# Start-up loads in two groups, a bias folded later, and experts' matrices in five slots, three tiles ahead

## The chip, the core and the metric

The kernel runs on one core of one Trainium2 chip. The metric is device time in microseconds (us) of one execution. All arrays are float32 in HBM; a few operands are bfloat16 in SBUF.

## The reference

The input is `x`, 32 sequences of 128 tokens with 128 features, and a context `ctx_1024` of the same shape. Four layers follow, each an attention and a feed-forward part, both added to `x`:

```python
x = x + xattn_l(layernorm(x), ctx, ...)     # l = 0..3
x = x + ffn_l(layernorm(x), ...)
```

- Layer 0 and 1: cross attention, 16 heads of 8 (causal in layer 0); then a mixture of 8 experts, of which each token takes 2 (128 to 512 to 128; ReLU, then GELU with biases).
- Layer 2: a decoder block (self attention, cross attention, a plain 128-512-128 network, three layer norms); then "gated attention": 8 experts that are attentions themselves, 2 for each token, with an output bias `ob` for each expert and a value bias `vb`. Attention weights add up to one, so `vb` goes through the output matrix unchanged: the kernel folds it into `ob` once, `ebias = ob + sum_p vbias_p^T Eo_p`.
- Layer 3: cross attention with rotary positions and a window of 64 tokens; then 8 experts with a gate (SiLU(x G) * (x U)) D, 2 for each token.

## The kernel before, in words

The 32 sequences are two streams, s = 0 and s = 1, of 16 sequences; a step works on a pair of sequences (256 tokens), so each stream has 8 pairs (`PAIRS`). Each stream is a Python generator for each engine. TensorE's generators give each step a cost and a delay; `choose_order` plays them against a model of time, starting stream 1 at `HEAD_START` = 100, and every engine then issues the steps of both streams in that one fixed order. So each engine is one in-order list with both streams interleaved.

Start. SyncE (SP) issues, in order: for both streams the first pair of `x` (`x_first`) and of the context (`c_in`); then 18 loads that all count on one semaphore, `weights_in`: `wproj` (all 52 projection matrices, 3328 KB) first, nine small tables, the masks, then seven tables spread over all partitions (`rows`, 960 KB, among them). TensorE, ScalarE and VectorE begin with a wait for all 18 (lines 338, 1098, 1332). VectorE then clears four PSUM banks and makes bfloat16 copies (lines 1334 to 1339); when `consts_set` is complete TensorE makes the bias fold (line 341, 8 products written as 16 instructions) and VectorE adds it to `ebias` (line 1342); both streams begin behind that. SP waits for `consts_set` too (line 798), since it then sends zeros from SBUF into stream 0's area for sorted rows, `sent` (line 794: four transfers of 2560 KB, `clear`), and only behind those, on the same queue, loads the other 14 sequences of `x` for each stream (line 802, `x_rest`, 896 KB each), and `wf`. VectorE needs `x_rest` early: in the third unit of pair 0's attention, `come` (line 1573) takes the statistics of pair 1 (line 1374).

Mixtures (layers 0, 1, 3; each stream; six in all). Tokens are scattered by expert into `sent`; VectorE makes a plan (`plan`) of 39 tiles (`TILES`) of 128 rows, each with its expert. For each tile SP reads the plan's registers and issues three transfers: the expert's matrices (line 845, `load_expert`: 512, 578 or 384 KB in layers 0, 1, 3), the tile's rows (line 849, `load_rows`, 64 KB) and the finished rows of tile n-2 (line 853, `store_rows`, 64 KB). In step n TensorE turns the rows of tile n (line 527), makes the first products of tile n-1 (`first`, line 535, 8 instructions) and the second ones of tile n-2 (`second`, line 543). VectorE or ScalarE take the results out; VectorE's copy of tile n-2's answer (line 1679 or 1681) releases SP, which then issues the load of tile n+2's expert into slot (n+2) mod 4, the slot that tile n-2 has left. Rows are loaded six tiles ahead. At a mixture's start two experts are loaded as soon as the plan is there (line 839 ff.), and the rows only when all scatters have landed.

After a mixture the answers come back by indirect DMA on GpSimd (line 958, `fetch`) and VectorE adds them (`combine`, line 1451). After the last mixture, stream 1's in layer 3, 8 pairs are fetched and stored; stream 0's last combines are interleaved with that mixture's tiles.

The bias fold is used in line 669, in the gated attention of layer 2.

## Time and profile before

| | |
|---|---|
| median of 3 runs | 3465.97 us (3463.64 to 3470.96) |
| the profiled execution, its own time | 3460.97 us |
| span of its trace | 3459.1 us |
| TensorE matmuls busy | 2811.5 us, 81% of the span |
| VectorE busy | 1986.3 us, 57% |
| ScalarE busy | 1326.2 us, 38% |
| GpSimd busy | 633.1 us, 18% |
| moved by DMA | 217.14 MB, mean 63 GB/s |

The span is 1.9 us shorter than the execution's own time, and that time is 5.0 us under the median. A share of busy time is a mean over very different stages. A "wait" is idle time of an engine just ahead of an instruction, with the event that ended it. "The chain" is the work followed back from the last instruction to what released each step. SPq is SP issuing DMAs. A transfer's bytes are moved by 16 DMA engines; "DMA share" is the mean share of these that is busy, and can be put a little over 1 in short stretches. PEclk is TensorE's granted clock; 1.00 is 2.4 GHz and 0.50 is 1.2 GHz.

### The profile page before, as it was taken

The page shows a single profiled execution, that of the slowest core. Times are in us where ns is not written, and L with a number is a line of the kernel's source. Part 1 is how long each engine was busy: PE and PEld are TensorE (multiplying, and loading weights), DVE is VectorE, ACT ScalarE, POOL GpSimd, SP SyncE. Part 2 cuts the span into 40 slices and gives each one's busy share as a digit, 9 for nine tenths or more (in the row PEclk, how much of TensorE's full clock was granted, in tenths as well). Part 3 has the DMA queues.
Part 4 walks back from the last instruction along what each step waited for, and adds up shares of the span by engine and source line. Part 5 has one row for each costly group of instructions (what it writes and reads, how often), then busy time and mean ns, then how long its engine had stood idle before and what let it go on. Part 6 is the DMA issues. An engine that isn't in the chain of part 4 may idle for free.

```text
span 3459.1 us, 64816 instructions
## 1 busy us (share of the span) xinstructions
PE 2811.5 (81%) x24730; PEld 1999.2 (58%) x24818; DVE 1986.3 (57%) x6642; ACT 1326.2 (38%) x3062; POOL 633.1 (18%) x847
## 2 busy tenths in 40 slices
PE   5888888866687997997988988988988988987852
PEld 2444666633574874664764765755655655656752
DVE  2566445456544355666666666666766766665432
ACT  1344334433474743333333333334334333334421
POOL 0122112223312011121121121111111111110033
PEclk8888998977797998999998999999999999998976
DMA  7300656500373810000000000000000000004464
GB/s 252 113 23 22 182 145 181 154 21 24 106 226 96 242 44 7 3 9 7 3 9 7 3 9 7 3 9 7 3 9 7 3 9 4 3 4 125 116 189 125
DMA packets 146515, 217.14 MB, mean 63 GB/s; under 512 B 20377, under 2 KB 99233, under 8 KB 146081
## 3 DMA queue, kind: packets, MB, share of 16 engines
q1 hardware_dynamic: 133920, 187.80, 17.8%
q0 software_dynamic: 12288, 25.19, 2.4%
q8 instruction: 200, 3.28, 0.4%
q14 instruction: 107, 0.87, 0.1%
HBM read 159.83 MB, written 53.08 MB: 62 GB/s over the span
## 4 chain that ended last, share of the span: by engine, by line
PE 56%; DVE 21%; ACT 10%; issue 6%; DMA 4%; SPq 2%; another core or an unknown queue 2%; POOL 1%; DVEq 0%; POOLq 0%; ACTq 0%
PE bank L442 5%; ACT ex L1132 5%; PE bank L380 5%; DVE mx L1594 4%; PE bank L535 4%; PE bank L617 4%; PE bank L386 4%; PE bank L452 4%; PE bank L599 3%; PE bank L462 3%; PE bank L543 3%; PE bank L371 3%; PE bank L446 3%; DMA expert<-in_moe 3%; PE bank L431 2%
## 5 line engine op out<-in xcount | busy, mean ns | idle before, releaser
L1132 ACT ACTIVATE ex<-bank 128x512 f32<-128x512 f32 x896 | 472.6, 600 | 661.1 <-PE bank L452 431.0
L1594 DVE TENSOR_REDUCE mx<-bank 128x4 bf16<-128x512 f32 x640 | 407.4, 683 | 125.3 <-PE bank L431 67.5
L944 POOL TENSOR_TENSOR rstd<-vare,power 128x2 f32<-128x2 f32 x192 | 135.8, 707 | 1372.9 <-DVE vare L1387 1372.9
L535 PE MATMUL bank<-qm,expert 128*128 128x128 f32 x1872 | 265.1, 287 | 35.6 <-DMA expert<-in_moe 29.4
L1011 POOL TENSOR_TENSOR oT<-oT 128x128 f32<-128x128 f32 x256 | 117.9, 461 | 917.2 <-DVE oT L1713 916.6
L535 PEld LDWEIGHTS bank<-qm,expert 128*128 128x128 f32 x1872 | 239.8, 200 | 51.8 <-DMA expert<-in_moe 39.4
L953 POOL DMA_INDIRECT sent<-tail_tok,pos x192 | 191.3, 996 | 391.5 <-DVE pos L1522 347.1
L380 PE MATMUL bank<-hT,wproj 128*128 128x256 f32 x736 | 242.8, 427 | 23.7 <-ACT hT L1095 8.3
L1586 DVE RECIPROCAL rden<-bank 128x16 f32<-128x16 f32 x160 | 41.0, 256 | 382.9 <-PE bank L471 347.2
L442 PE MATMUL bank<-qm,kf 32*128 32x512 f32 x1280 | 207.4, 710 | 56.8 <-ACT ex L1132 36.0
L617 PEld LDWEIGHTS bank<-ev,ex 128*128 128x128 f32 x2048 | 246.9, 192 | 5.1 <-issue 0.2
L425 PE MATMUL bank<-km,qb 32*128 32x512 bf16 x640 | 141.3, 447 | 133.4 <-DVE logit L1463 33.4
L617 PE MATMUL bank<-ev,ex 128*128 128x65 f32 x2048 | 243.7, 272 | 0.0
L543 PE MATMUL bank<-expert,hid 128*128 128x128 f32 x1560 | 220.4, 281 | 20.7 <-DVE hid L1667 11.4
L452 PEld LDWEIGHTS bank<-identb,mx 128*128 128x128 bf16 x2560 | 160.3, 102 | 89.5 <-issue 58.6
L543 PEld LDWEIGHTS bank<-expert,hid 128*128 128x128 f32 x1560 | 197.2, 195 | 25.6 <-DVE hid L1667 12.2
L462 PE MATMUL bank<-ex,vaug 128*9 128x128 f32 x5120 | 185.2, 275 | 21.4 <-issue 9.9
L371 PE MATMUL bank<-masks,identb 128*128 128x512 bf16 x648 | 179.8, 415 | 20.1 <-issue 11.1
L1699 DVE TENSOR_REDUCE emax<-bank 128x4 bf16<-128x512 f32 x256 | 164.3, 683 | 46.4 <-PE bank L589 46.1
L452 PE MATMUL bank<-identb,mx 128*128 128x128 bf16 x2560 | 179.7, 226 | 9.0 <-DVE mx L1594 9.0
L1091 ACT ACTIVATE oT<-bank 128x512 f32<-128x512 f32 x160 | 96.0, 600 | 194.6 <-PE bank L462 150.3
L425 PEld LDWEIGHTS bank<-km,qb 32*128 32x128 bf16 x640 | 33.9, 93 | 216.6 <-issue 141.0
(207 smaller groups left out, 5051.0 us busy)
## 6 DMA issues: line engine op xcount, KB each, us to landing
expert<-in_moe SPq DMA_DIRECT2D x78, 578.0 KB
expert<-in_moe SPq DMA_DIRECT2D x78, 512.0 KB
expert<-in_moe SPq DMA_DIRECT2D x78, 384.0 KB
sent<-zeros SPq DMA_DIRECT2D x8, 2560.0 KB, 9.1
ex<-sent SPq DMA_DIRECT2D x234, 64.0 KB
answered<-qm SPq DMA_DIRECT2D x234, 64.0 KB
ctxT<-ctx_kept SPq DMA_DIRECT2D x32, 128.0 KB
wproj<-in_wproj SPq DMA_DIRECT2D x1, 3328.0 KB
```

The source lines that it names most:

```text
L371: nc.tensor.matmul(ps[:], identb[:, 0, :], masks[:], start=True, stop=True)
L380: mm = nc.tensor.matmul(ps[:, n * NT:(n + 1) * NT], W(weight), src[:], start=True, stop=True)
L425: mm = nc.tensor.matmul(ps[i][:], qb[s][r, seq(b)], km[s][r, :, seq(b)], start=True, stop=mask is None)
L442: nc.tensor.matmul(ps[j][:], kf[s][band_rows(j), seq(b)], qm[s][band_rows(j), :, seq(b)], start=True, stop=False)
L452: mm = nc.tensor.matmul(ps[j][:, i * P:(i + 1) * P], mx[s][:, b, h:h + 1].to_broadcast([P, P]), identb[:, 1, :], start=False, stop=i == HB ...
L462: mm = nc.tensor.matmul(ps[32 * i:32 * i + D + 1, j * P:(j + 1) * P], vaug[s][:, b, HB * j + i, :], ex[s][:, j, i, :], start=True, stop=True)
L535: mm = nc.tensor.matmul(ps[:, chunk(c)], expert[s][:, t % SLOTS, chunk(c)], t_turned[s][:, t % 2, :], start=True, stop=True)
L543: mm = nc.tensor.matmul(ps[:, 0:P], t_hid[s][:, t % 2, chunk(c)], expert[s][:, t % SLOTS, 512 + c * P:512 + (c + 1) * P], start=c == 0, st ...
L617: mm = nc.tensor.matmul(ps[:, c * (HE + 1):(c + 1) * (HE + 1)], ex[s][:, 2 * (p % 2) + i, 2 * b + j, :], ev[s][:, p % 2, b, i, :], start=T ...
L953: nc.gpsimd.indirect_dma_start(sent[s][:], bass.IndirectOffsetOnAxis(ap=pos[s][:, i, j:j + 1], axis=0), tail_tok[s][:, j // 2, :], None).t ...
L1132: give(nc.scalar.activation(ex[s][:, i], ps[:].rearrange("p (i q) -> p i q", i=4), ACT.Exp, scale=SCALE), *key)
L1594: give(nc.vector.tensor_reduce(mx[s][:, b, HB * i:HB * i + HB], ps[:].rearrange("p (i k) -> p i k", i=HB), AX.X, ALU.max), *k, "s", b, i)
```

## The change

Three parts.

1. SP issues first the first pair of stream 0, then six transfers on a new semaphore `first_weights_in` (`ident`, `band`, `cols`, the masks, the first four projection matrices, 256 KB, and `rows`), then the first pair of stream 1, then the other loads, among them the remaining 48 projection matrices, on `weights_in`. TensorE, ScalarE and VectorE begin after `first_weights_in`. Waits for `weights_in` stand ahead of the first router product on TensorE and ahead of the first gates on VectorE. VectorE clears the PSUM banks before its wait. Bytes, and the number of transfers but for one more, stay the same.
2. The bias fold leaves the start. Stream 0 makes it once behind its mixture of layer 1, in a PSUM bank of the ring "g"; VectorE adds it there.
3. Five slots for experts in place of four, and `EXPERTS_AHEAD = 3`: at a mixture's start three experts are loaded, and after tile n-2's answer is out SP loads the expert of tile n+3 (slot (n+3) mod 5, the slot that tile n-2 has left). The event that releases a load is the same as before.

```diff
--- before.py
+++ after.py
@@ -55,7 +55,8 @@
 PLANNED = -(-TILES // BATCH) * BATCH
 
 MOE_COLS = {0: 512 + CH * P, 1: 512 + CH * P + CH + P, 3: 3 * CH3 * P}
-SLOTS = 4
+SLOTS = 5
+EXPERTS_AHEAD = 3
 
 ROW_SLOTS = 8
 ROWS_AHEAD = 6
@@ -102,7 +103,7 @@
     + [f"{n}{s}_{i}" for n in ("expert_in", "last_in") for s in range(STREAMS) for i in range(SLOTS)] \
     + [f"rows_in{s}_{i}" for s in range(STREAMS) for i in range(ROW_SLOTS)] \
     + [f"rows_out{s}_{i}" for s in range(STREAMS) for i in range(OUT_SLOTS)] \
-    + ["weights_in", "ffn_weights_in", "consts_set", "bias_made", "bias_in", "dve_step"]
+    + ["first_weights_in", "weights_in", "ffn_weights_in", "consts_set", "bias_in", "dve_step"]
 CONSTS = 20
 
 PROJ = ["L0q", "L0k", "L0v", "L0o", "L1q", "L1k", "L1v", "L1o", "L2q1", "L2k1", "L2v1", "L2q2", "L2k2",
@@ -112,6 +113,10 @@
 ROWS = ["L0v", "L0o", "L1v", "L1o", "L2v1", "L2v2", "L3v", "L3o", "g1", "be1", "g2", "be2", "g3", "be3",
         "bf2"]
 ROUTERS = {0: 0, 1: 1, 3: 2}
+FIRST_PROJ = 4
 
 
 class Counts:
@@ -296,10 +301,12 @@
         eq_bf16 = [[eq[s][i].rearrange("p i n -> p (i n)").bitcast(BF16)[:, 1::2].rearrange("p (i n) -> p i n", i=2)
                     for i in range(3)] for s in range(STREAMS)]
 
-        loads = [(wproj, "wproj"), (router, "router"), (rw1, "rw1"), (rw2, "rw2"), (cols, "cols"), (rope, "rope"),
-                 (ident, "ident"), (band, "band"), (ebias, "ebias"), (vbias, "vbias")]
-        spread = [(rows, "rows"), (rrow, "rrow"), (rb2, "rb2"), (tri, "tri"), (region, "region"),
-                  (tile_rows, "tile_rows"), (tile_no, "tile_no")]
+        first_loads = [(ident, "ident"), (band, "band"), (cols, "cols")]
+        n_first = len(first_loads) + 3
+        loads = [(router, "router"), (rw1, "rw1"), (rw2, "rw2"), (rope, "rope"), (ebias, "ebias"), (vbias, "vbias")]
+        spread = [(rrow, "rrow"), (rb2, "rb2"), (tri, "tri"), (region, "region"), (tile_rows, "tile_rows"),
+                  (tile_no, "tile_no")]
         n_loads = len(loads) + len(spread) + 1
         masks_f32 = hid[0][:, 0, 0:3, :].rearrange("p a n -> p (a n)")[:, 0:5 * P].rearrange("p (m k) -> p m k", m=5)
 
@@ -335,12 +342,8 @@
         @block.tensor
         def _(pe):
             w = Counts()
-            pe.wait_ge(sem["weights_in"], 16 * n_loads)
+            pe.wait_ge(sem["first_weights_in"], 16 * n_first)
             pe.wait_ge(sem["consts_set"], CONSTS)
-            for p in range(HP):
-                mm = nc.tensor.matmul(bank[6][0:NE, 0:P], vbias[:, p, :], W(f"Eo{p}"), start=p == 0, stop=p == HP - 1)
-            mm.then_inc(sem["bias_made"], 1)
-            pe.wait_ge(sem["bias_in"], 1)
 
             def open_bank(ring, *key):
                 i, n = banks.fill(ring, key)
@@ -396,6 +399,8 @@
                     turn(t, tail_tok[s], "tT")
 
                 def tail_logits(t):
+                    if w.new("weights_in", 16 * n_loads):
+                        pe.wait_ge(sem["weights_in"], 16 * n_loads)
                     taken(*t, "tT")
                     by_token(t, "logits", router[:, ROUTERS[tail_layer(t[2])], :], attT[s], NE)
 
@@ -663,6 +668,8 @@
                             turn_mixed(n - 3)
                         yield "gated unit", 3.6 if 2 <= n < HP else 2.5 if n <= HP + 1 else 0.3, 0.3 if n <= HP else 1.5
                     taken(*k, "wtsT")
+                    if w.new("bias_in", 1):
+                        pe.wait_ge(sem["bias_in"], 1)
                     taken(*k, f"mixedT{HP - 1}")
                     for b in range(NB):
                         ps = open_bank("g", *k, "out", b)[:, 0:P]
@@ -708,6 +715,11 @@
                 yield from mixture((s, "M", 1))
 
 
+                if s == 0:
+                    ps = open_bank("g", "ebias")
+                    for p in range(HP):
+                        mm = nc.tensor.matmul(ps[0:NE, 0:P], vbias[:, p, :], W(f"Eo{p}"), start=p == 0, stop=p == HP - 1)
+                    filled(mm, "ebias")
                 yield "gather", 0.0, 9.0
                 for i in range(PAIRS):
                     tail = (s, i - 1, "C") if i else None
@@ -780,12 +792,21 @@
         @block.sync
         def _(sp):
             w = Counts()
-            for s in range(STREAMS):
+            def first_pair(s):
                 sp.dma_start(x_tok[s][:, 0:NB, :], x_dram[s, :, 0:NB, :]).then_inc(sem[f"x_first{s}"], 16)
                 sp.dma_start(c_st[s][:], c_dram[s, 0]).then_inc(sem[f"c_in{s}"], 16)
+            first_pair(0)
+            for dst, src in first_loads:
+                sp.dma_start(dst[:], A[src]).then_inc(sem["first_weights_in"], 16)
+            sp.dma_start(masks_f32, A["masks"]).then_inc(sem["first_weights_in"], 16)
+            sp.dma_start(wproj[:, 0:FIRST_PROJ, :], A["wproj"][:, 0:FIRST_PROJ, :]).then_inc(sem["first_weights_in"], 16)
+            sp.dma_start(rows[:], A["rows"].unsqueeze(0).to_broadcast(list(rows.shape)))\
+                .then_inc(sem["first_weights_in"], 16)
+            first_pair(1)
             for dst, src in loads:
                 sp.dma_start(dst[:], A[src]).then_inc(sem["weights_in"], 16)
-            sp.dma_start(masks_f32, A["masks"]).then_inc(sem["weights_in"], 16)
+            sp.dma_start(wproj[:, FIRST_PROJ:, :], A["wproj"][:, FIRST_PROJ:, :]).then_inc(sem["weights_in"], 16)
             for dst, src in spread:
                 sp.dma_start(dst[:], A[src].unsqueeze(0).to_broadcast(list(dst.shape))).then_inc(sem["weights_in"], 16)
 
@@ -856,7 +877,7 @@
                     at = {}
                     sp.wait_ge(sem[f"plan_ready{s}"], w.next(f"plan_ready{s}"))
                     read_plan(0)
-                    for t in range(2):
+                    for t in range(EXPERTS_AHEAD):
                         load_expert(t)
                     sp.wait_ge(sem[f"scattered{s}"], sent_off)
                     read_plan(BATCH)
@@ -866,8 +887,8 @@
                     for n in range(TILES + 2):
                         if n >= 2:
                             taken(*k, "y", n - 2)
-                        if n + 2 < TILES:
-                            load_expert(n + 2)
+                        if n + EXPERTS_AHEAD < TILES:
+                            load_expert(n + EXPERTS_AHEAD)
                         if n >= 2:
                             store_rows(n - 2)
                         if n + ROWS_AHEAD < TILES:
@@ -1074,7 +1095,7 @@
         @block.scalar
         def _(act):
             w = Counts()
-            act.wait_ge(sem["weights_in"], 16 * n_loads)
+            act.wait_ge(sem["first_weights_in"], 16 * n_first)
             act.wait_ge(sem["consts_set"], CONSTS)
             def take(*key):
                 i, n = banks.fills[key]
@@ -1329,17 +1350,15 @@
         @block.vector
         def _(dve):
             w = Counts()
-            dve.wait_ge(sem["weights_in"], 16 * n_loads)
             for i in (4, 5, 6, 7):
                 nc.vector.memset(bank[i][:], 0.0).then_inc(sem["consts_set"], 1)
+            dve.wait_ge(sem["first_weights_in"], 16 * n_first)
             nc.vector.tensor_copy(masks[:], masks_f32[:, 0:4, :]).then_inc(sem["consts_set"], 1)
             nc.vector.tensor_copy(countb[:, 0, :], masks_f32[:, 4, :]).then_inc(sem["consts_set"], 1)
             nc.vector.tensor_copy(identb[:, 0, :], ident[:]).then_inc(sem["consts_set"], 1)
             nc.vector.tensor_scalar(identb[:, 1, :], ident[:], -1.0, None, ALU.mult).then_inc(sem["consts_set"], 1)
             nc.vector.memset(pad[:], 0.0).then_inc(sem["consts_set"], 1)
             dve.wait_ge(sem["consts_set"], CONSTS)
-            dve.wait_ge(sem["bias_made"], 1)
-            nc.vector.tensor_tensor(ebias[:], ebias[:], bank[6][0:NE, 0:P], ALU.add).then_inc(sem["bias_in"], 1)
 
             def settle(ins):
                 ins.then_inc(sem["dve_step"], 1)
@@ -1456,6 +1475,8 @@
                     dve.wait_ge(sem[f"combined{s}"], w.next(f"combined{s}"))
 
                 def gates_in(k, bias=False, by_slot=False):
+                    if w.new("weights_in", 16 * n_loads):
+                        dve.wait_ge(sem["weights_in"], 16 * n_loads)
                     lg = take(*k, "logits")[:, 0:NB * NE].rearrange("p (b e) -> p b e", b=NB)
                     if bias:
                         ins = nc.vector.tensor_tensor(logit[s][:], lg, over_seqs(rb2[:]), ALU.add)
@@ -1795,6 +1816,10 @@
                 yield from last_tail((s, PAIRS - 1, "B"))
                 yield from mixture((s, "M", 1))
 
+                if s == 0:
+                    ps = take("ebias")
+                    settle_given(nc.vector.tensor_tensor(ebias[:], ebias[:], ps[0:NE, 0:P], ALU.add), "ebias")
+                    nc.vector.memset(pad[:], 0.0).then_inc(sem["bias_in"], 1)
                 yield "gather"
                 for i in range(PAIRS):
                     x = rows_of(i)
```

## Rows read from the trace of the kernel before

**Rows 1.** The page: busy time of the engines, and the chain by engine.
```profile
PE 2811.5 (81%) x24730; PEld 1999.2 (58%) x24818; DVE 1986.3 (57%) x6642; ACT 1326.2 (38%) x3062; POOL 633.1 (18%) x847
...
PE 56%; DVE 21%; ACT 10%; issue 6%; DMA 4%; SPq 2%; another core or an unknown queue 2%; POOL 1%; DVEq 0%; POOLq 0%; ACTq 0%
```
**Rows 2.** The chain in order of time, 0 to 80 us: start us, us, what.
```profile
37.53 19.81 DMA x_tok<-in_x
```
**Rows 3.** Timeline, 0 to 75 us: start, duration, engine, line, operation, [idle before].
```profile
8.18 3.59 SPq L788 DMA_DIRECT2D hid<-in_masks  x1
...
23.38 14.12 SPq L794 DMA_DIRECT2D sent<-zeros  x4
...
23.50 3.57 PE L341 MATMUL bank<-wproj,vbias 128*8 128x128 f32 x16 [23.50 <-DVE pad L1339]
...
57.37 0.48 DVE L1374 BATCH_NORM_STATS2 stats<-x_tok 128x6 f32<-128x128 f32 x2 [17.09 <-DMA x_tok<-in_x]
```
**Rows 4.** Waits of SP's queue, 0 to 70 us: total us, times, longest.
```profile
SPq L794 <- DVE pad L1339: 8.0, 1, 8.0
```
**Rows 5.** Stretches at the start: length, busy by engine, PEclk, DMA share, GB/s.
```profile
16.00:20.00 4.00, 0.00 (x0) 0.00 (x0) 0.00 (x0) 0.00 (x0) 0.00 (x0) 1.00 0.56 192
20.00:23.00 3.00, 0.00 (x0) 0.00 (x0) 2.34 (x7) 0.00 (x0) 0.00 (x0) 1.00 0.00 0
23.00:27.00 4.00, 3.50 (x16) 1.98 (x16) 0.33 (x4) 0.00 (x0) 0.00 (x0) 1.00 0.68 248
```
**Rows 6.** Waits of the whole span, those of TensorE for experts' matrices.
```profile
PEld bank L535 <- DMA expert<-in_moe: 39.4, 40, 3.8
...
PE bank L535 <- DMA expert<-in_moe: 29.4, 34, 3.6
```
**Rows 7.** The same waits, 3290 to 3459 us, the last mixture.
```profile
PEld bank L535 <- DMA expert<-in_moe: 31.9, 26, 3.8
PE bank L535 <- DMA expert<-in_moe: 25.5, 25, 3.6
```
**Rows 8.** Timeline in the last mixture, around 3360 us.
```profile
3358.70 1.16 PE L535 MATMUL bank<-qm,expert 128*128 128x128 f32 x8 [0.54 <-DMA expert<-in_moe]
...
3358.92 0.33 SPq L845 DMA_DIRECT2D expert<-in_moe  x1
...
3360.29 1.16 PE L535 MATMUL bank<-qm,expert 128*128 128x128 f32 x8
...
3362.67 1.16 PE L535 MATMUL bank<-qm,expert 128*128 128x128 f32 x8 [0.67 <-DMA expert<-in_moe]
```
**Rows 9.** Timeline: the first products of the fourth and of the last tile there.
```profile
3317.31 1.91 PE L535 MATMUL bank<-qm,expert 128*128 128x128 f32 x8
...
3405.78 1.16 PE L535 MATMUL bank<-qm,expert 128*128 128x128 f32 x8 [0.61 <-DMA expert<-in_moe]
```
**Rows 10.** Stretch 3317 to 3407 us, line 535 alone: length, PE, PEld, PEclk, DMA share, GB/s.
```profile
3317.00:3407.00 90.00, 45.29 (x288) 39.43 (x288) 0.92 0.78 227
```
**Rows 11.** DMA of the stretch 3316 to 3404 us.
```profile
DMA packets 16995, 19.96 MB, mean 227 GB/s; under 512 B 1968, under 2 KB 12336, under 8 KB 16987
```
**Rows 12.** A stretch of 10 us in the last mixture, columns as in rows 5.
```profile
3340.00:3350.00 10.00, 7.23 (x57) 6.19 (x55) 3.45 (x13) 2.92 (x9) 3.77 (x4) 1.00 0.87 261
```
**Rows 13.** The chain in order of time: its pieces without a known releaser within mixtures.
```profile
362.01 3.56 another core or an unknown queue
...
1063.64 7.89 another core or an unknown queue
...
3301.54 13.55 another core or an unknown queue
...
3333.49 2.92 another core or an unknown queue
```
**Rows 14.** Timeline, TensorE behind stream 0's mixture of layer 1.
```profile
1072.21 1.11 PE L471 MATMUL bank<-ident,oT 128*128 128x128 f32 x4 [8.11 <-ACT oT L1091]
```
**Rows 15.** Timeline, TensorE in a gated attention: 16 instructions over 8 output matrices.
```profile
1461.80 2.05 PE L671 MATMUL bank<-wproj,hid 128*128 128x128 f32 x16
```

## The prediction

> **What bounds the kernel now.** I read the page first: TensorE is busy 81% of the span, and 56% of the chain is its work [rows 1]. Over most of the span, then, only less TensorE work or fewer of its waits make the kernel faster. DMA holds a few per cent of the chain; the question is where. I read the start, the mixtures and the end apart.
>
> The start: the chain holds one piece of 19.81 us, from the issue of `x_rest` to its landing at 57.34 [rows 2]. VectorE stood idle 17.09 us for it [rows 3], and TensorE with it. So what sets the end of the start is not `weights_in` and not the bias fold, but a load that stands behind four clears on SP's queue. These are issued at 23.38, behind an 8.0 us wait for `consts_set` [rows 3, 4]. Meanwhile the 16 engines run dry: share 0.56 in 16 to 20 us, 0.00 in 20 to 23, 0.68 in 23 to 27 [rows 5].
>
> The mixtures: the table of waits puts 29.4 us of idle TensorE (39.4 for the weight loads, which run ahead) on experts' matrices [rows 6]; 25.5 (31.9) of these lie in the last mixture, where no other stream fills TensorE [rows 7]. The page's lines of the chain put more on these loads; but the chain counts a load from its issue, and only the wait can be won.
>
> The end after it (8 fetches, 3409 to 3459 us) is untouched.
>
> **Part 1, the order of the loads.** Pair 0 of stream 0 starts when six small transfers and `rows` are in, instead of all 18; then it comes to the same wait for `x_rest` and only waits longer. The value is what `x_rest` gains. Its queue has the same bytes ahead; what changes is how long the engines are idle before it lands.
> - Removed: SP's 8.0 us wait. The new `consts_set` needs only the first group. I put it at about 11 us: its last transfer is issued near 5 us, as the issues come some 0.5 us apart while the queue is short, then come 1.9 MB and four copies of VectorE. SP ends the issues at 12 to 16 us. So the clears follow the loads with no hole: idle engine time won = 4 x 0.44 + 3 x 1.00 + 4 x 0.32 = 1.8 + 3.0 + 1.3 = 6.1 us [rows 5].
> - Added: the 3328 KB matrix load, which kept the engines full from 4 us on (SP even stood 3.59 us at the masks, its queue being full [rows 3]), now comes at 9 to 10 us. Before it go some 2.4 MB, about 6 us of transfers in some 8.5: 2.1 to 2.7 us idle, new.
> - Sum: 6.1 - 2.1 = 4.0 us earlier. Bounds: 2 (more holes among the small transfers) and 6.1 (none). SP's context copy and the load of pair 1's context stand behind `x_rest` and `wf` on the queue and move with it.
>
> **Part 2, the bias fold.** At the start it goes: 3.57 us on TensorE [rows 3] and VectorE's addition. Gain 0, since both lie before the 17.09 us wait; if that cover were gone, it would be some 3.9 us. It comes back behind stream 0's mixture of layer 1: 16 instructions, 2.05 us at the full clock by the like products of line 671 [rows 15], 3.57 as it was at the low one [rows 3]. Behind it on TensorE wait stream 1's units, and VectorE waits for it in order. A gap of 7.89 us with no known releaser on ScalarE's side, in which TensorE stands 8.11 us, comes a few us later [rows 13, 14] and may swallow it. Cost between 0 and 3.9; I take 2.0, full clock and not hidden. Using one more bank of ring "g" shifts all later uses alike. The two waits for `weights_in` cost nothing: they come a pair later, when those loads are long in.
>
> **Part 3, five slots.** The releasing event (VectorE's copy of tile n-2) and the bytes stay; each load gets one more tile of time. In the last mixture two tiles' first products follow in 1.59 us when nothing is waited for (3358.70 to 3360.29), while a load issued at 3358.92 is used at 3362.67 behind a wait of 0.67: 3.75 us, landing included [rows 8]. Two tiles ahead cover 2 x 1.59 - 0.22 = 2.96 us, three cover 4.55. So 3.75 is covered by three and not by two. But the transfers may then bound the stage: from tile 4 to the last there are 35 periods in 88.5 us, 2.53 us each [rows 9], with 288 / 8 = 36 tiles of instructions [rows 10]. The stage moved 19.96 MB in 88 us [rows 11] at 227 GB/s and a share of 0.78 [rows 10], so 291 GB/s at share 1: 68.6 us at least, 78.8 at the share of 0.87 that it reaches now for 10 us [rows 12]. TensorE alone would need 36 x 1.59 = 57. So the transfers are next in line: gain 88 - 78.8 = 9.2 to 88 - 68.6 = 19.4. I take 13, a share of 0.92, nearer the reached one, since 10 us of the stage run at the low clock and single holes remain. Bounds: 4 (only the two waits of over 3 us go) and 19.4.
>
> In the other five mixtures TensorE's waits for these loads are 29.4 - 25.5 = 3.9 us, by the weight loads 39.4 - 31.9 = 7.5 [rows 6, 7]. TensorE is the bound there, so they count in full: I take 4, bounds 0 and 7.5. The third load at each mixture's start goes ahead of the rows: 384 KB at 291 GB/s is 1.4 us, in the time in which SP waits for the scatters; nothing.
>
> The Trainium skill, DMA: Bandwidth & Descriptors, section "Anatomy of one DMA", gives a transfer (issued by GpSimd, not SP) about 2.0 us and its bytes at 436 GB/s; for 384 KB that is an estimate of 2.9 us, by which two tiles ahead would suffice; the trace disagrees, with its 3.75 us.
>
> **The sum.** -4 (start) + 2 (fold) - 4 (five mixtures) - 13 (last mixture) = -19 us. Against the profiled execution: its span 3459.1 becomes 3440, its own time 3461.0 becomes 3442. The median lies 5.0 us above that execution, and I move it by as much: 3465.97 - 19 = 3447.
>
> **The rivals.**
> - A: transfers bound the last mixture already. For it: the share is 0.87 at best over 10 us, and single engines may be full while the mean isn't. Against it: at the start the same engines reach 1.0 and more, and a load is waited for while others finish in 3 to 4 us. Then part 3 gains 4 there and 2 in the other five: -4 + 2 - 2 - 4 = -8, 3458. Chance 0.17.
> - B: two tiles ahead cover a load, or the fifth slot changes nothing that TensorE waits for (the change doesn't do what it says). Then only the start is left: -4 + 2 = -2, 3464. Against it stand the waits of rows 7. Chance 0.04. The page's rule named above is this one.
> - C, slower: the gaps without a known releaser grow. In the mixtures they are 3.56, 7.89, 13.55 and 2.92 us, 27.9 in all [rows 13]: ScalarE has its operands and starts late. The page shows a queue for instructions on the same 16 engines; if that is what is late, a third load in front delays it. It would decide if these gaps doubled in all mixtures: -19 + 27.9 = +9, 3475. Against it: the bytes per us rise by some 15% (13 of 88 us), not twofold. Chance 0.05.
> - D: the same gaps shrink, or the transfers fill to the full and the fold is hidden: -4 - 7 - 19 = -30 to -36, 3430 to 3436. The gaps depend on what meets what on the queues, and all is shifted by 4 us or more after the start. Chance 0.14.
>
> The Trainium skill, Runtime: NRT & Kernel Launch, section "Instruction fetch mechanics", has engines fetch the next 16 KiB of instructions while they run the current ones, mostly hidden. By it the gaps of rows 13 are no fetches and C falls away; the trace shows the gaps, not their cause.
>
> **How the numbers follow.** Forecast -19: chance 0.60. Its own range by the bounds is -2 - 0 - 4 + 3.9 = -2 to -6 - 7.5 - 19.4 = -33; not all ends come together. The range 3431 to 3461 takes in A and most of D and leaves out B and C and little more. A difference under 0.2% (7 us) can't be told from none in a measurement of this kernel. Faster by more: nearly all of the forecast and D, two thirds of A: 0.85. Within 0.2%: the rest of A, B, some of C: 0.10. Slower: 0.05.
>
> **What would show it.** Start: VectorE's statistics of pair 1 at 53 instead of 57.4 us, no 8.0 us wait of SP, no stretch with share 0 after 10 us, and a wait for `x_rest` that is longer (near 28 us). Fold: 16 products around 1055 us, 2 us, and the gap behind them 8 or 6 us long. Mixtures: line 535's waits for experts down from 29.4 to under 12 us, all in the last mixture; its share near 0.92, its 35 periods in some 75 us instead of 88.5. I'd be wrong if that share stayed at 0.8 (A), if `x_rest` landed no earlier, or if the pieces without releaser came to over 45 us.

## The result, and the profile after

The changed kernel took 3434.95 us (median of 6 runs, 3429.03 to 3449.58), the kernel before, beside it on the same chip, 3458.89 us. The ratio is 0.9934 with a 95% interval of 0.9907 to 0.9961, or -23 us by the ratio where -19 were forecast; its size in later measurements is taken up below. The profiled execution of after took 3449.58 us, its span is 3447.8 us.

The page of after, the head, the busy time, the chain by engine, and the costliest line of the experts' products (columns as in its legend: busy, mean ns of one, idle before):

```profile
span 3447.8 us, 64821 instructions
...
PE 2817.4 (82%) x24730; PEld 1996.0 (58%) x24818; DVE 1989.0 (58%) x6643; ACT 1326.8 (38%) x3062; POOL 635.1 (18%) x847
...
PE 58%; DVE 21%; ACT 10%; issue 5%; another core or an unknown queue 2%; SPq 2%; DMA 1%; POOL 1%; DVEq 0%; POOLq 0%; ACTq 0%
...
L540 PE MATMUL bank<-qm,expert 128*128 128x128 f32 x1872 | 260.2, 283 | 16.9 <-DMA expert<-in_moe 9.3
```

The work is the same as in [rows 1]. DMA's part of the chain fell from 4% to 1%, and TensorE's rose from 56% to 58%: that is what fewer waits for loads look like on the page.

The start. First the piece of the chain that answers to [rows 2], then timeline rows (start, duration, engine, line, operation, [idle before]) that answer to [rows 3]:

```profile
34.68 18.57 DMA x_tok<-in_x
```
```profile
3.20 0.43 SPq L802 DMA_DIRECT2D hid<-in_masks  x1
...
11.26 0.43 DVE L1356 CAST masks<-hid 128x512 bf16<-128x512 f32 x1 [8.24 <-DMA rows<-in_rows]
...
13.52 21.12 SPq L815 DMA_DIRECT2D sent<-zeros  x4
...
34.68 14.29 SPq L823 DMA_DIRECT2D x_tok<-in_x  x2
...
53.27 0.49 DVE L1393 BATCH_NORM_STATS2 stats<-x_tok 128x6 f32<-128x128 f32 x2 [26.80 <-DMA x_tok<-in_x]
```

The statistics of pair 1 stand at 53.27 instead of 57.37 us: 4.1 us earlier. VectorE now waits 26.80 us for them instead of 17.09, as pair 0 is done earlier. The clears are issued from 13.52 us on, and the 8.0 us wait of [rows 4] is gone. Note that the four clears take SP 21.12 us to issue, where a small transfer takes 0.43: it stands in them while the 16 engines are busy to 1.05 (27 to 40 us). I read that as a full queue; the trace shows the long issues, not the queue's state.

The lead of 4.1 us doesn't last at once. At GpSimd's fifth root behind pair 0 (a root is its power instruction in a normalization) after is ahead by only 1.4 us (110.59 against 112.00), and by 4.1 again at 283 us.

The stretches of [rows 5], same columns:

```profile
16.00:20.00 4.00, 3.53 (x12) 1.74 (x11) 2.08 (x7) 0.84 (x2) 0.00 (x0) 1.00 0.88 317
20.00:23.00 3.00, 1.54 (x7) 0.34 (x6) 1.29 (x2) 2.30 (x5) 0.00 (x0) 0.91 0.36 94
23.00:27.00 4.00, 4.00 (x12) 0.59 (x10) 2.58 (x4) 0.00 (x0) 0.00 (x0) 0.50 1.05 409
```

The stretch without any transfer is gone, but not the whole hole: 0.36 in 20 to 23 us.

TensorE's waits for experts in the whole span (total us, times, longest), which answer to [rows 6, 7]; none of them lies outside the last mixture any more:

```profile
PEld bank L540 <- DMA expert<-in_moe: 15.5, 20, 1.6
...
PE bank L540 <- DMA expert<-in_moe: 9.3, 14, 1.4
```

The last mixture: the stretch around it with line 540 alone, then the DMA head of 3322 to 3394 us, then 10 us of it with all lines, and last the first products of the last tile. They answer to [rows 10], [rows 11], [rows 12] and [rows 9]:

```profile
3322.00:3397.00 75.00, 41.38 (x288) 35.91 (x288) 0.97 0.88 267
```
```profile
DMA packets 17105, 19.90 MB, mean 276 GB/s; under 512 B 1982, under 2 KB 12489, under 8 KB 17097
```
```profile
3340.00:3350.00 10.00, 7.97 (x68) 7.34 (x66) 4.96 (x17) 3.20 (x10) 4.04 (x5) 1.00 0.96 295
```
```profile
3323.63 0.63 PE L540 MATMUL bank<-qm,expert 128*128 128x128 f32 x2
...
3394.31 1.06 PE L540 MATMUL bank<-qm,expert 128*128 128x128 f32 x8
```

The 35 periods from tile 4 to the last take 3394.31 - 3323.63 = 70.7 us instead of 88.5: 17.8 us less, with the same bytes.

The bias fold and the gap behind it (timeline; the middle row is the chain's piece that answers to [rows 13], the last one answers to [rows 14]):

```profile
1049.85 1.91 PE L721 MATMUL bank<-wproj,vbias 128*8 128x128 f32 x16
```
```profile
1055.97 6.01 another core or an unknown queue
```
```profile
1062.66 1.11 PE L476 MATMUL bank<-ident,oT 128*128 128x128 f32 x4 [4.88 <-ACT oT L1112]
```

The fold takes 1.91 us, and the gap behind it is 6.01 us long instead of 7.89.

**Where the two profiled executions part.** I took the same instruction in both traces, such a root, and subtracted its starts. After is ahead by 4.1 us at the first root of pair 1, by 11.2 at the start of layer 2 (1257.21 against 1246.05), then behind by 6.3 at the end of layer 2 (3278.86 against 3285.17), and ahead by 11.5 at the first products of the last tile, which is about the difference of the spans (11.3). So layer 2 took 17.5 us more in this execution of after. The change has no part in it but the addition of the fold's result, and the table of waits shows no new wait there. What differs in the profile is the granted clock: its mean over layer 2 (the column after the five engines) is 0.94 in before and 0.93 in after.

```profile
1257.20:3278.90 2021.70, 1755.55 (x15502) 1234.14 (x15562) 1303.72 (x4183) 750.69 (x1668) 309.92 (x480) 0.94 0.06 16
```
```profile
1246.00:3285.20 2039.20, 1772.51 (x15502) 1238.95 (x15562) 1304.96 (x4183) 751.68 (x1668) 310.95 (x480) 0.93 0.06 16
```

The number of TensorE's instructions is the same (x15502), and their busy time is 17.0 us longer. By the records of the clock, TensorE was at the lower level for 257.8 us of layer 2 in before and for 296.6 us in after. Whether that belongs to the change is a question for the experiments.

### The profile page after: what moved, and what is told of

Same layout as the page of the kernel before. It is cut to its first block, busy times and chain, and to the rows that moved or that the text cites. A ratio compares the mean times of both kernels' runs of the same rounds, so it can differ in the third digit from the quotient of the medians.

```text
span 3447.8 us, 64821 instructions
## 1 busy us (share of the span) xinstructions
PE 2817.4 (82%) x24730; PEld 1996.0 (58%) x24818; DVE 1989.0 (58%) x6643; ACT 1326.8 (38%) x3062; POOL 635.1 (18%) x847
## 3 DMA queue, kind: packets, MB, share of 16 engines
q1 hardware_dynamic: 134064, 187.80, 17.8%
## 4 chain that ended last, share of the span: by engine, by line
PE 58%; DVE 21%; ACT 10%; issue 5%; another core or an unknown queue 2%; SPq 2%; DMA 1%; POOL 1%; DVEq 0%; POOLq 0%; ACTq 0%
PE bank L447 5%; PE bank L383 5%; ACT ex L1153 5%; PE bank L540 4%; PE bank L622 4%; DVE mx L1615 4%; PE bank L548 4%; PE bank L389 3%; PE bank L604 3%; PE bank L467 3%; PE bank L457 3%; PE bank L451 3%; PE bank L436 3%; PE bank L374 2%; PE bank L430 2%
## 5 line engine op out<-in xcount | busy, mean ns | idle before, releaser
L548 PE MATMUL bank<-expert,hid 128*128 128x128 f32 x1560 | 219.0, 280 | 25.3 <-DVE hid L1688 13.7
L457 PEld LDWEIGHTS bank<-identb,mx 128*128 128x128 bf16 x2560 | 158.6, 101 | 98.7 <-issue 58.1
L548 PEld LDWEIGHTS bank<-expert,hid 128*128 128x128 f32 x1560 | 194.9, 194 | 31.2 <-DVE hid L1688 14.6
```

Source lines behind the costliest of these rows:

```text
L457: mm = nc.tensor.matmul(ps[j][:, i * P:(i + 1) * P], mx[s][:, b, h:h + 1].to_broadcast([P, P]), identb[:, 1, :], start=False, stop=i == HB ...
L548: mm = nc.tensor.matmul(ps[:, 0:P], t_hid[s][:, t % 2, chunk(c)], expert[s][:, t % SLOTS, 512 + c * P:512 + (c + 1) * P], start=c == 0, st ...
```

## The experiments

My theory: start -4, fold up to +2, five mixtures -4, last mixture -13 or more, bounded next by the transfers; layer 2's clock is chance. The rivals: the gain comes from one part alone; the fifth slot and not the lead makes it; the low clock in layer 2 is caused by the change. In the table, "root 1" and "root 5" are the starts of GpSimd's first and fifth root behind pair 0, "last" is the length from the first products of tile 4 to those of the last tile in the last mixture, "wait" is TensorE's wait for experts' matrices in the whole span, "low" is layer 2's time at the lower clock level, and "layer 2" is the length of layer 2. These marks are of one profiled execution each, all in us. Chips differ, so "before" is that of the same chip: e1 to e4 ran on one chip, e5 to e8 on another, e9 to e12 on a third; which chip had the first measurement is not on record. "One run" means a single execution and no interval.

| kernel | time | before | ratio (95%) | root 1 / 5 | last | wait | low / layer 2 |
|---|---|---|---|---|---|---|---|
| e1 changed again | 3437.57 | 3456.66 | 0.9946 (0.9920 to 0.9971) | 53.6 / 110 | 73.5 | 9.5 | 277 / 2031 |
| e2 start and fold | 3459.05 | 3456.66 | 1.0004 (0.9979 to 1.0029) | 54.3 / 110.9 | 83.6 | 28.2 | 297 / 2039 |
| e3 slots alone | 3443.94 | 3456.66 | 0.9964 (0.9936 to 0.9991) | 58.1 / 114.4 | 72.0 | 8.2 | 314 / 2048 |
| e4 x_rest ahead | 3433.64 | 3456.66 | 0.9918 (0.9892 to 0.9945) | 27.3 / 104.2 | 71.8 | 9.2 | 280 / 2035 |
| e5 clears later | 3329.93 | 3386.6 | 0.9831 (0.9817 to 0.9844) | 27.4 / 83.7 | 71.2 | 14.6 | 287 / 2019 |
| e6 four ahead | 3350.11 | 3386.6 | 0.9913 (0.9881 to 0.9945) | 54.6 / 106.3 | 66.9 | 8.9 | 239 / 2006 |
| e7 5 slots, 2 ahead | 3380.21 | 3386.6 | one run | 53.6 / 105.7 | 85.9 | 31.4 | 246 / 2010 |
| e8 half loads | 3347.04 | 3386.6 | one run | 53.5 / 107.9 | 66.7 | 9.7 | 239 / 2006 |
| e9 as changed | 3427.13 | 3442.61 | one run | 53.4 / 107.1 | 72.7 | 6.9 | 267 / 2026 |
| e10 later, four ahead | 3401.68 | 3442.61 | 0.9861 (0.9828 to 0.9894) | 27.4 / 88.4 | 69.7 | 5.9 | 287 / 2029 |
| e11 changed, beside e10 | 3429.06 | 3442.61 | 0.9948 (0.9921 to 0.9975) | 53.5 / 109.8 | 72.7 | 7.4 | 259 / 2023 |
| e12 before, half loads | 3431.98 | 3442.61 | one run | 58.9 / 112.7 | 76.7 | 13.7 | 231 / 2014 |

### The changed kernel again, and its parts alone

e1 is the changed kernel without an edit.

> The changed kernel unaltered, beside the kernel before on the same chip. If the low-clock stretches of layer 2 that the first profile showed are chance, this profile shows another sum of them (between 690 and 730 us of PEclk 0.5 over the span, unrelated to the change), and the ratio is again near 0.9935 (-20 to -25 us). If the change itself costs clock in layer 2, the stretch from the end of the mixtures of layer 1 to the last mixture is again some 15 us longer than before's. In either case the first statistics of pair 1 stand near 53.3 us and the last mixture takes 70 to 73 us from tile 4 to the last.

Measured: ratio 0.9946. The gain is there again, at -19 us, and with e11 on another chip at -14. e1, e9 and e11 run the same program as after, and layer 2 took 2031, 2026 and 2023 us in them against 2039 in the first profile, with 277, 267 and 259 us at the lower clock level against 297. So most of the 17.5 us of the first profile came with that execution. But all four are longer than the one profile of before (2022 us), and e12, the kernel before with half loads, has 2014 on the chip of e9 and e11. These profiles can't exclude a cost of a few us.

The mean granted clock of all executions says more. On the chip of e1 it is 0.8991 in the changed kernel (11 executions) and 0.9033 in before (35), with a standard error of 0.0010 for the difference; beside e11 0.9020 (9) and 0.9054 (14). e2 has 0.8991 (12), e3 0.9028 (12), e4 0.9031 (11). Taken as time at the lower level over the span, these are 694 us for e1 and 698 for e2, against 668 for before, 670 for e3 and 665 for e4. So a lower clock does go with the new start and the fold (e1, e2, e11), not with the slots (e3), and it is gone again in e4, whose `x_rest` comes early. Why is not shown. Part of it costs nothing: in after TensorE stands still from 35.4 to 54.9 us, and the clock is at the lower level from 39.5 to 70.2, so 15.4 us of that fall into the standstill, against 4.1 in before. Within the 35 executions of before, length grows by 0.34 us with each us at the lower level; for the 15 of the 26 us that are left this is an estimate of 5 us, too few to be told from none here.

e2 keeps the order of loads and the later fold, and takes the slots back:

```diff
-SLOTS = 5
-EXPERTS_AHEAD = 3
+SLOTS = 4
+EXPERTS_AHEAD = 2
```

> Parts 1 and 2 alone (four slots, two tiles ahead). My account: x_rest lands near 53.3 us (-4.1), the fold costs up to 2 us, the last mixture is as before (88 us from tile 4 to the last, waits of line 535 some 25 us): -2 to -4 us in all. The rival, that loads ahead are worth nothing and the start gives all: -20 us or more.

e3 is the kernel before with the slots alone:

```diff
-SLOTS = 4
+SLOTS = 5
+EXPERTS_AHEAD = 3
@@
-                    for t in range(2):
+                    for t in range(EXPERTS_AHEAD):
                         load_expert(t)
@@
-                        if n + 2 < TILES:
-                            load_expert(n + 2)
+                        if n + EXPERTS_AHEAD < TILES:
+                            load_expert(n + EXPERTS_AHEAD)
```

> Part 3 alone on the kernel before. My account: start as before (57.4 us), TensorE's waits for experts from 29.4 to under 12 us, last mixture 70 to 73 us instead of 88: -17 to -22 us. The rival that transfers bound that mixture already: -4 to -8 us. The sum of this one and parts 1 and 2 alone should be the whole change, if they don't interact.

Waits of e2, then of e3:

```profile
PE bank L540 <- DMA expert<-in_moe: 28.2, 33, 1.9
DVE stats L1393 <- DMA x_tok<-in_x: 27.0, 1, 27.0
```
```profile
DVE stats L1375 <- DMA x_tok<-in_x: 16.4, 1, 16.4
...
PE bank L536 <- DMA expert<-in_moe: 8.2, 14, 1.1
```

Each part does its own work and not the other's: e2 has the earlier start (root 1 at 54.3 instead of 58.1 us) and the old waits for experts, e3 the old start and the short waits. In time, the first can't be told from nothing (1.0004, the -2 us of the sum being 0.9994), and the slots carry the gain (0.9964). That is -12.5 us, less than the 17 to 22 expected, though the interval's end, 0.9936, is -22. The product 0.9968 lies inside e1's interval: no interaction is needed.

### What holds the start now

e4 issues the first stream's `x_rest` ahead of the four clears (`rest(s)` holds the load of `x_rest` for one stream):

```diff
             sp.wait_ge(sem["consts_set"], CONSTS)
+            rest(0)
             for part in range(CLEARINGS):
                 clear(0, part)
-            for s in range(STREAMS):
-                sp.dma_start(x_tok[s][:, NB:, :], x_dram[s, :, NB:, :]).then_inc(sem[f"x_rest{s}"], 16)
+            rest(1)
```

> The changed kernel with stream 0's x_rest issued ahead of its four clears and stream 1's behind them. If x_rest behind the clears is what ends the start, its 26.8 us wait goes but for the landing of 0.9 MB behind the loads: pair 1's statistics near 27 us instead of 53, and 20 to 27 us less in all against the changed kernel, as long as the clears are done before the first scatter. The rival, that something else of the start stands right behind (the clears now late for the scatter, which waits for them, or the context loads that queue behind them): the wait moves to pair 1's context or the scatter, and under 8 us is won.

The timeline of e4, SP and the product that waits:

```profile
12.36 0.44 SPq L820 DMA_DIRECT2D x_tok<-in_x  x1
12.85 25.21 SPq L815 DMA_DIRECT2D sent<-zeros  x4
38.10 6.82 SPq L820 DMA_DIRECT2D x_tok<-in_x  x1
44.96 7.80 SPq L828 DMA_DIRECT2D wf<-in_wf  x2
...
53.28 0.43 SPq L907 DMA_DIRECT2D c_st<-in_ctx  x1
```
```profile
58.54 0.69 PE L366 MATMUL bank<-ident,c_st 128*128 128x128 f32 x2 [19.66 <-DMA c_st<-in_ctx]
```

Root 1 comes 26 us earlier than in e1, but root 5 only 6, and the time is 4 us less. The wait moved: SP stands in its own issues (25.21 + 6.82 + 7.80 us) and so gives out the load of pair 1's context only at 53.28 us, for which TensorE then waits 19.66 us. The rival in the expectation is what happened.

e5 also puts the clears, the second stream's `x_rest` and `wf` behind pair 0's context store and load (added lines alone; they are gone from their old place):

```diff
             sp.wait_ge(sem["consts_set"], CONSTS)
+            rest(0)
@@
                     if i + 1 < PAIRS:
                         sp.dma_start(c_st[s][:], c_dram[s, i + 1]).then_inc(sem[f"c_in{s}"], 16)
+                    if s == 0 and i == 0:
+                        for part in range(CLEARINGS):
+                            clear(0, part)
+                        rest(1)
+                        for n in wf:
+                            sp.dma_start(wf[n][:], A[n]).then_inc(sem["ffn_weights_in"], 16)
```

> The changed kernel with stream 0's x_rest first and its four clears, stream 1's x_rest and wf issued only behind pair 0's context store and pair 1's context load. In the run before, the wait had moved to pair 1's context, whose load SP could issue only at 53.3 us. If the fill of SP's queue by the clears is all that holds the start, pair 1's statistics stay near 27 us, its context waits under 2 us, the mark of the fifth root (110.6 us in the changed kernel, 104.2 with x_rest first) comes near 85 us, and the whole is 20 to 27 us faster than the changed kernel, near 3412. The rival: the scatter of pair 0, which waits for all clears, or pair 2's context is late next: then under 12 us are won against the changed kernel.

```profile
23.18 0.43 SPq L902 DMA_DIRECT2D c_st<-in_ctx  x1
23.66 14.98 SPq L815 DMA_DIRECT2D sent<-zeros  x4
```
```profile
27.36 0.69 POOL L969 TENSOR_TENSOR rstd<-vare,power 128x2 f32<-128x2 f32 x1 [14.43 <-DVE vare L1410]
...
83.70 0.69 POOL L969 TENSOR_TENSOR rstd<-vare,power 128x2 f32<-128x2 f32 x1 [12.42 <-DVE vare L1410]
```

The context load leaves at 23.18 us instead of 53.28, and root 5 stands at 83.70 us, 22.6 before that of e6, which has the changed kernel's start on the same chip. In time e5 is 20 us under e6, although e6 loads four tiles ahead. The four clears (10240 KB), which nobody needs before the first scatter, cost over 20 us as long as they stood ahead of small loads that were needed at once. The changed kernel itself has no run on this chip. Against before the ratio comes to -57 us, more than the change's 14 to 23 and this step's 22.6 make together. The clock may be in it: e5's executions have a mean of 0.9132, before beside them 0.9080.

### What holds the last mixture

e7 keeps five slots but loads two tiles ahead (`EXPERTS_AHEAD = 2`).

> Five slots, but two tiles ahead. If the lead is what wins, the last mixture is as in the kernel before: 84 to 90 us from tile 4 to the last, 25 us of waits. If the free slot itself wins (a load that no longer meets a slot just left), it is near 71 us.

```profile
PE bank L540 <- DMA expert<-in_moe: 31.4, 29, 2.5
```
```profile
SPq L866 <- DVE qm L1702: 20.3, 12, 2.6
```

The last mixture takes 85.9 us, as with four slots (83.6 in e2, 88.5 in before). The slot alone does nothing; the lead makes the gain. The second row (SP's own waits in this mixture) tells why: SP stands ready 20.3 us for VectorE's copy of tile n-2, and then issues a load that is late. In after the same wait is short:

```profile
SPq L866 <- DVE qm L1702: 2.1, 4, 1.1
SPq L874 <- DVE qm L1702: 1.4, 2, 1.2
```

SP waits 3.5 us of some 71; the rest of the time it issues and moves registers.

e6 gives layer 3 six slots in the same room (its columns are 768 of at most 1156) and loads four ahead:

```diff
+SLOTS_OF = {0: SLOTS, 1: SLOTS, 3: 6}
+AHEAD_OF = {0: EXPERTS_AHEAD, 1: EXPERTS_AHEAD, 3: 4}
@@
-                        if n + EXPERTS_AHEAD < TILES:
-                            load_expert(n + EXPERTS_AHEAD)
+                        if n + AHEAD_OF[layer] < TILES:
+                            load_expert(n + AHEAD_OF[layer])
```

> The changed kernel with, in layer 3 only, six slots and four tiles ahead (the same room, as its matrices are narrower). If transfers bound the last mixture with three ahead (its share of the 16 engines is 0.95), one more tile ahead wins under 2 us of the 70.7 and the share stays at 0.93 to 0.97. If latency still bounds it, the stretch from tile 4 to the last falls to 62 to 66 us and line 540's waits to under 3 us.

It takes 66.9 us against 71.2 in e5 (three ahead) on that chip, with waits of 8.9 against 14.6 us. The stretch, all lines:

```profile
3225.00:3291.80 66.80, 56.62 (x456) 51.54 (x454) 31.47 (x100) 22.97 (x70) 19.92 (x22) 1.00 0.95 298
```

Neither expectation was met: 4.3 us are more than the 2 of transfers as the bound, and neither the length nor the waits fell as far as a bound by latency would have it. The share is 0.95, but the rate is 298 GB/s, above the 291 that the prediction worked out for share 1: full share is no fixed number of bytes, and 291 GB/s was no ceiling.

e8 is the changed kernel with half the bytes. It leaves out the second half of each layer 3 expert's columns: the slot keeps what was there.

```diff
-                    cols_ = MOE_COLS[layer]
+                    cols_ = 384 if layer == 3 else MOE_COLS[layer]
@@
-                        sp.dma_start(expert[s][:, t % SLOTS, 0:cols_], A[f"moe{layer}"][bass.ds(at[t][1], P), :])\
+                        sp.dma_start(expert[s][:, t % SLOTS, 0:cols_], A[f"moe{layer}"][bass.ds(at[t][1], P), 0:cols_])\
```

> The changed kernel, in layer 3 loading only the first 384 of 768 columns of each expert; the rest of the slot holds what was there, so layer 3's experts compute with other numbers, the same instructions. Bytes of the last mixture fall from 19.9 to some 13 MB. If transfers bound it with three ahead, tile 4 to the last falls from 70.7 to 58 to 61 us (TensorE's 1.59 us a tile and a few single waits) and the waits for experts to under 2 us. If it were bound by something else, it stays within 3 us of 70.7.

The last mixture of e8, all lines (columns as in [rows 5]); and SP's issues over four tiles in it, those of line 874 and all but one of line 870 left out:

```profile
3225.00:3291.00 66.00, 56.13 (x450) 52.17 (x449) 29.56 (x98) 22.93 (x70) 20.82 (x23) 0.97 0.74 207
```
```profile
3250.38 0.33 SPq L866 DMA_DIRECT2D expert<-in_moe  x1
...
3251.95 0.33 SPq L866 DMA_DIRECT2D expert<-in_moe  x1
...
3253.45 0.33 SPq L866 DMA_DIRECT2D expert<-in_moe  x1
...
3254.95 0.33 SPq L866 DMA_DIRECT2D expert<-in_moe  x1
...
3256.76 0.34 SPq L870 DMA_DIRECT2D ex<-sent  x1
3257.44 0.40 SPq L941 DMA_DIRECT2D out_x<-x_tok  x1
3258.04 0.33 SPq L866 DMA_DIRECT2D expert<-in_moe  x1
```

The mixture takes 66.7 us, not the 58 to 61 that I expected; I had taken the transfers for the next bound and TensorE's 57 us for the one behind it. With a third of the bytes gone (13.65 MB against 19.90) the share falls to 0.74, and only some 4 us are won against e5 or after. SP's row of issues says why. In this mixture SP waits 0.3 us in all. Its loads follow each other in 1.50 us where it only issues three transfers, and in 3.09 us where it also reads the plan and issues a store of the output: 7.66 us for four tiles, 1.92 each, so 67 us for 35 of them, and 66.7 were measured. In e8, then, SP's own list is the bound. e6 moves all the bytes over the same list and takes 66.9 us, with 2.2 us of SP's waits: it stands at the same floor, so with four tiles ahead it was most likely the list too, and not the transfers, that set the time.

e9 was meant to raise that cost: one more read of the plan in the three of four steps of layer 3 that have none, the same values into the same registers.

```diff
                         if n + ROWS_AHEAD < TILES:
                             if (n + ROWS_AHEAD) % BATCH == 0:
                                 read_plan(n + ROWS_AHEAD)
+                            elif layer == 3:
+                                reread(n + ROWS_AHEAD)
                             load_rows(n + ROWS_AHEAD)
```

> The changed kernel, but in layer 3 SyncE reads the tile plan again (the same values into the same registers) in each step of a mixture, not in every fourth: three quarters of its steps get one more read. Nothing else moves, and no byte is added to a queue. Theory (after the change the last mixture is held by SyncE's own row of issues, about 1.5 us for three of them and the registers' moves, and 0.7 us more where the plan is read; the two stages of waits recur every fourth tile): each of some 22 to 26 extra reads costs up to its 0.7 us, the last mixture grows from 70 to 74 us to 82 to 92, the waits of its first matmuls for expert from about 10 to 18 or more. Rival (transfers or TensorE hold it, SyncE has room between its issues): it stays at 70 to 75 us with waits of about 10 us in some 14 places. The rest of the kernel as in the changed kernel.

It says nothing on the question: its trace holds the same 60 reads of tables into SP's registers as that of e11, so the added ones never ran (I take it that they were dropped as having no use; that isn't shown). So e9 ran the changed kernel once more, and its 72.7 us are those of a repeat. That SP's list bounds the last mixture rests on e8's rows and on e6's equal length; for three tiles ahead with full loads it was not tested.

e12 takes half of the bytes from the kernel before, by the same edit as e8. It leaves out the same columns.

> The kernel before (four slots, two tiles ahead), but in layer 3 each load brings only the first 384 of an expert's 768 columns; the rest of its slot keeps what was there. It tells the two bounds of the kernel before apart. If two tiles ahead were too short because the bytes in the queue take long (a load of 384 KB 3.75 us alone, more in the queue): with half the bytes the last mixture falls from 86 to 88 us to 70 to 75 and the waits for expert from about 30 us in 30 places to 10 to 15. If the load's fixed time and SyncE's stalls ahead of its issue, not the bytes, held it, it stays at 82 us or more.

```profile
PE bank L535 <- DMA expert<-in_moe: 13.7, 21, 2.7
```
```profile
3300.00:3376.00 76.00, 60.96 (x449) 54.93 (x450) 31.11 (x102) 22.63 (x70) 15.09 (x16) 0.94 0.64 175
```

76.7 us lie between the two expectations, a little nearer to the first. With two tiles ahead, half the bytes bring 7 to 12 us (83.6 in e2, 85.9 in e7, 88.5 in before, none of them measured beside e12), so the time of a load in the queue did hold that kernel. At the same half bytes, three ahead (e8) are 10 us shorter. Not all of that is the lead: the waits for experts differ by 4 us (13.7 and 9.7), and e12's chain holds 3.91 us without a known releaser in this mixture, where e8's, on its chip, has none. Still, with 21 waits of up to 2.7 us left, a lead of two tiles doesn't cover even a load of half the size.

### Both steps together

e10 is e5's start with e6's longer lead; e11 is the changed kernel beside it.

> The changed kernel with both steps that won alone: the clears of sent, the second stream's x_rest and the layer's weights stand behind pair 0's context store and load, and layer 3 has six slots loaded four tiles ahead. If the two act in separate places (start and last mixture) their gains add: the mark of the first GpSimd root at 27 us and the fifth at 84 (changed kernel 54 and 107 to 110), the last mixture at 67 us (71 to 73), the time 4 us under that of the later clears alone, so 1.7 to 2.0% under the kernel before (ratio 0.980 to 0.983). If the longer lead only gave back what the clock took elsewhere, the ratio is that of the later clears alone, 0.9831, or above.

> The changed kernel itself, beside the others on their chip. Theory: ratio 0.9905 to 0.996, last mixture 70 to 74 us, first root at 54 us; the difference to the later clears with longer lead is 1.0 to 1.5%. If the gain of the change were the chance of a few executions, its ratio would lie within 0.998 to 1.002.

The fifth roots of e10 and of e11:

```profile
88.43 0.70 POOL L973 TENSOR_TENSOR rstd<-vare,power 128x2 f32<-128x2 f32 x1 [12.42 <-DVE vare L1414]
```
```profile
109.83 0.70 POOL L965 TENSOR_TENSOR rstd<-vare,power 128x2 f32<-128x2 f32 x1 [13.16 <-DVE vare L1406]
```

e10 takes 3401.68 us, 41 under the kernel before and 27 under the changed kernel on the same chip, so both edits together beat both kernels. The start gives 21.4 us of these 27, as read at root 5. The longer lead gives 3 us in the last mixture (69.7 against 72.7). The other 3 have no place that I can name. The ratio, 0.9861, is above the 0.980 to 0.983 that I expected from e5's 0.9831, though its interval reaches 0.9828; the same start was worth 21.4 us at root 5 here and 22.6 there, so the difference isn't in the start. In mean granted clock e10 is nearly level with before beside it (0.9063 and 0.9054), while e5 was above (0.9132 and 0.9080). At 0.34 us for each us at the lower level that is an estimate of 10 of the 16 us by which e5's gain is larger. Whether four ahead add anything to the time of e5 stays open.

## Why the prediction came out, step by step

- **Start, -4.** Measured -4.1 in the profile, -3.8 in e2 against e3 (54.3 and 58.1 us). The mechanism was right: the 8.0 us wait is gone, and idle engine time with it. That the size came out so exactly is in part luck, as its two terms were both off. Of the old hole (6.1 us) 2.4 stayed, at shares of 0.88 in 16 to 20 us and 0.36 in 20 to 23. The new hole among the small transfers was about 0.8 us and not 2.1 to 2.7: shares of 0.04, 0.62 and 0.83 in the first three stretches of 2 us, against 0.06, 0.83 and full in before. Both together account for 2.9 of the 4.1 us.
- **Fold, +2 (0 to 3.9).** It takes 1.91 us at the full clock, as forecast. In the first profile nothing of it shows: ahead of the fold, at the roots near 1026 us, after is ahead by 8.5 us, and behind it, near 1106, by 9.2; the gap behind the fold was 1.88 us shorter, so it swallowed the fold. In e2 against e3 the same stretch came out 3.3 us longer instead. The term stays as uncertain as it was written, and neither sign is shown.
- **Five other mixtures, -4.** TensorE's waits for experts there fell from 3.9 us to nothing. From the first root to the start of layer 2 after gained 7.1 us more, the fold and five mixtures included; by the forecast it was to be 2. Two executions can't resolve what lies above that.
- **Last mixture, -13.** It gained 17.8 us in the first pair of profiles. Over all profiles with full loads, two tiles ahead took 83.6, 85.9 and 88.5 us, three ahead 70.7 to 73.5 (seven profiles, mean 72.1): a gain of 13.9 between the means. So mechanism and size were right, and the first pair had the longest and the shortest of its kind. The floor under it was wrong. 68.6 us rested on 291 GB/s at share 1, and e6 moved the same bytes at 298 GB/s in 66.9 us. As a theory of what stands next the transfers were at least incomplete, too: with 0.69 of the bytes the stage still took 66.7 us (e8).
- **The sum, -19.** -23 us beside the first measurement, -19 and -14 on the chips of e1 and e11. In the first profiled pair the spans differ by 11.3 us only: -4.1 at the start, -7.1 to layer 2, +17.5 in layer 2, -17.8 in the last mixture, +0.2 behind it. The third of these was no term of the sum; by e1, e9 and e11 it was mostly that one execution, and what the change itself costs there is not shown to be nothing. So start, other waits and last mixture, about 22 us together, are shown stage by stage, and the fold and the clock, which take from them, are not resolved.
- **Rival A** (transfers bound already, gain 4) fell by the last mixture's 17.8 us. **Rival B** (two ahead are enough, or the slot changes nothing) fell by e7: its slot without its lead left 85.9 us. The Trainium skill, DMA: Bandwidth & Descriptors, section "Anatomy of one DMA", by which the estimate for one load was 2.9 us, fits one DMA that GpSimd issues. In a queue of SP's, with the engines busy to 0.82, e7 shows that a lead of two tiles is too short.
- **Rivals C and D** (the pieces without a known releaser double or shrink): [rows 13] had 3.56, 7.89, 13.55 and 2.92 us, 27.9 in all. After has these:

```profile
358.01 3.59 another core or an unknown queue
...
3308.28 13.13 another core or an unknown queue
...
3344.55 2.25 another core or an unknown queue
```

With the 6.01 us behind the fold (shown above) and one more of 2.31 us in the last mixture these are 27.3 us. A third load in front neither lengthened nor shortened them. Outside the mixtures the chain of after has four such pieces in the attention of layer 1, 15.2 us instead of 3.3, but its lead over before grew by 0.6 us in that stretch, so they cost nothing: the chain only ran over another branch. Two facts narrow what they are. On the chip of e5 to e8 there are none: neither the chain nor any wait of ScalarE or VectorE has an unknown releaser in these four traces, though e7 differs from e1 in the lead alone. There the kernel before took 3386.6 us, against 3442.6 to 3458.9 in the other measurements. So the pieces are no property of the program. And the queue for instructions moved no packet during the pieces of 13.13, 6.01 and 3.59 us in after, so C's mechanism, a late fetch, has no support in the trace. The Trainium skill, Runtime: NRT & Kernel Launch, section "Instruction fetch mechanics", calls the cost of fetches mostly hidden; the trace agrees as far as these pieces go. What ends them stays open.

## What to carry to other kernels

Where a stage waits for loads that are released by its own progress, count the lead in tiles against the measured time of a load in the busy queue, and spend a slot only together with a longer lead. Look next at what the issuing engine has to do per tile: once it no longer waits, its list of issues is a floor (67 us here). And at the start of a kernel, order one queue by when each transfer is needed: the change moved 4 us there, and 21 more lay in clears that stood ahead of two small loads; moving only one of these ahead just moved the wait to the other.

## What I had not expected of the hardware

- TensorE's granted clock over the same instructions differs from execution to execution. Layer 2 has 231 to 314 us at the lower level in the kernels of this study, and its length follows: 2014 us at 231 (e12), 2023 at 259 (e11), 2039 at 297 (after), 2048 at 314 (e3). About 0.4 us of length went with each us at the lower level. On the chip of e5 to e8, which is without the pieces of unknown releaser, it is shorter: 2019 at 287 (e5). Four executions of one program lie 16 us apart in this stage, nearly as much as the whole gain of the change, so the two single traces had to be compared stage by stage.
- The four clears of 2560 KB took SP 21.12 us to issue in after and 25.21 us in e4. In before each issue of a load in the last mixture took 0.33 us [rows 8]. While SP stood in such an issue it gave out nothing that was behind it, loads on other semaphores included: in e4 the 0.43 us issue of pair 1's context came only at 53.28 us.
- With nothing to wait for, three issues and their register moves cost SP 1.50 us (e8), close to the 1.59 us that TensorE needs for a tile [rows 8].
- Nearly the same programs run without any piece of unknown releaser on one chip (e5 to e8), and with some 35 to 60 us of them in the chain in the ten other traces. A kernel's gaps can belong to the chip that it was profiled on.
